# Splitting the expert weights earlier and later in a cross-attention and mixture-of-experts kernel

## The reference

```python
x = x + xattn(layernorm(x), ctx, ctx, mask, Wq, Wk, Wv, Wo)   # 16 heads of 8, softmax over 64 keys
flat = layernorm(x).reshape(2048, 128)
top_scores, top_idx = top_k(flat @ router_w.T + router_bias, 2)
combine[n, top_idx] = softmax(top_scores)
up, gate = einsum('nd,kde->nke', flat, up_proj), einsum('nd,kde->nke', flat, gate_proj)
down = einsum('nke,ked->nkd', silu(gate) * up, down_proj)
x = x + einsum('nk,nkd->nd', combine, down) + (silu(flat @ sh_gate.T) * (flat @ sh_up.T)) @ sh_down.T
```

## Time and profile before

| | us |
|---|---|
| median of 3 runs | 188.59 (188.44 to 189.77) |
| the profiled execution, its own time | 188.98 |
| its span, first to last instruction | 187.2 |
| PE busy | 168.3 (90%) |
| DVE busy | 162.1 (87%) |
| ACT busy | 123.4 (66%) |
| POOL busy | 81.0 (43%) |

### The profile page before, as it was taken

The page is one execution under the profiler, slowest core; times in us unless marked ns, Lnnn a source line. Parts: engine busy times, 40 slices in busy tenths (PEclk is TensorE's granted clock), DMA queues, the critical chain, the costliest instruction groups (busy, mean ns, idle before and its releaser), DMA issues.

```text
span 187.2 us, 4388 instructions
## 1 busy us (share of the span) xinstructions
PE 168.3 (90%) x1512; PEld 131.6 (70%) x1512; DVE 162.1 (87%) x436; ACT 123.4 (66%) x282; POOL 81.0 (43%) x145
## 2 busy tenths in 40 slices
PE   7586798998989899889999989999999999999962
PEld 7554556665767677666777668888888878888841
DVE  6899999698989999988992998998998899889961
ACT  2293567686888888888889566475566555665531
POOL 5765993558688888797663523030000000000000
PEclk9999999999999999999999999999999999999995
DMA  5997700000000000001400222422554254614401
GB/s 135 315 242 187 298 12 4 2 4 2 4 0 4 0 5 0 4 0 59 158 23 0 60 105 73 121 102 87 138 173 124 71 139 127 157 72 142 81 0 56
DMA packets 13060, 15.37 MB, mean 82 GB/s; under 512 B 1520, under 2 KB 8048, under 8 KB 12912
## 3 DMA queue, kind: packets, MB, share of 16 engines
q1 hardware_dynamic: 12608, 14.57, 26.6%
q10 hardware_dynamic: 432, 0.55, 1.2%
HBM read 13.93 MB, written 1.18 MB: 81 GB/s over the span
## 4 chain that ended last, share of the span: by engine, by line
PE 39%; DVE 32%; ACT 10%; POOL 10%; issue 6%; DMA 2%; DVEq 0%; ACTq 0%
PE bank L1105 31%; DVE prob L804 5%; DVE smax L802 5%; PE bank L1058 4%; ACT prob L564 3%; POOL k_blk L435 3%; DVE v_all L842 3%; DVE xn L704 3%; POOL w_lo L462 2%; DVE xn L700 2%; DVE hid L880 2%; POOL rstd L469 2%; DVE stats L690 2%; DMA x_sb<-x 2%; ACT hid_hi L634 2%
## 5 line engine op out<-in xcount | busy, mean ns | idle before, releaser
L625 ACT ACTIVATE sig<-bank 128x512 f32<-128x512 f32 x36 | 21.6, 600 | 21.8 <-PE bank L1105 21.4
L1105 PE MATMUL bank<-xt_hi,w_hi 128*128 128x512 f32 (+1 forms) x72 | 29.2, 406 | 0.0
L1105 PE MATMUL bank<-xt_lo,w_hi 128*128 128x512 f32 (+1 forms) x72 | 28.4, 394 | 0.0
L1105 PE MATMUL bank<-xt_hi,w_lo 128*128 128x512 f32 (+1 forms) x72 | 28.2, 391 | 0.0
L863 DVE TENSOR_TENSOR hid_u<-sig,bank 128x512 f32<-128x512 f32 x32 | 21.9, 685 | 4.3 <-PE bank L1105 3.1
L804 DVE TENSOR_TENSOR prob<-bank,smax 128x512 f32<-128x512 f32 x32 | 22.1, 692 | 1.1
L1058 PE MATMUL bank<-k_blk,q_blk 64*128 64x256 f32 x128 | 18.1, 402 | 5.3 <-POOL k_blk L435 4.7
L559 ACT COPY prob_t<-bank 128x512 f32<-128x512 f32 x32 | 17.3, 589 | 8.3 <-PE bank L1034 8.3
L802 DVE TENSOR_REDUCE smax<-bank 128x8 f32<-128x512 f32 x32 | 21.8, 681 | 0.8 <-PE bank L1058 0.8
L564 ACT ACTIVATE prob<-prob 128x512 f32<-128x512 f32 x32 | 20.1, 628 | 1.1 <-DVE prob L804 0.7
L872 DVE TENSOR_TENSOR hid_lo<-hid,hid_hi 128x512 fp32r<-128x512 f32 x24 | 16.6, 690 | 1.3 <-ACT hid_hi L634 0.5
(11 more groups left out here) (113 smaller groups left out, 383.4 us busy)
## 6 DMA issues: line engine op xcount, KB each, us to landing
mix_all<-w_rows SPq DMA_DIRECT2D x64, 128.0 KB, 3.0
w_moe_sb<-w_moe SPq DMA_DIRECT2D x1, 1728.0 KB, 10.3
x_sb<-x SPq DMA_DIRECT2D x4, 256.0 KB, 7.1
ctxt_sb<-ctx_t SPq DMA_DIRECT2D x4, 256.0 KB, 6.0
ctx_sb<-ctx_nat SPq DMA_DIRECT2D x4, 256.0 KB, 5.1
out<-x_sb SPq DMA_DIRECT2D x3, 256.0 KB, 2.3
w_att_sb<-w_att ACTq DMA_DIRECT2D x1, 272.0 KB, 6.4
mrow<-mask_row ACTq DMA_DIRECT2D x1, 256.0 KB, 5.2
```

The source lines that it names most:

```text
L625: nc.scalar.activation(sig[r][:, :], gate_ps[r][:, :], ACT.Silu).then_inc(s_sig, 1)
L1105: last = nc.tensor.matmul(out, w, moving, start=start and k == 0, stop=stop and k == 2)
```

## The change

The 16 pairs of a high and a low slice stay what they are, and each has one ACT and one POOL instruction as before; they stand elsewhere in the lists. ACT rounds slices 0 to 5 behind the key copy of group 2 in the projection (and waits there until the weights have landed), slices 6 and 7 behind the key copy of group 3, and slices 8 to 15 at the end of steps 0 to 7. POOL forms the low slices 0 to 5 behind the blocks of tile 1, 6 and 7 in step 0, 8 to 10 in step 14, 11 to 13 in step 15, and 14 and 15 behind the last but one `norm2`. The waits for the last queries and keys move behind the first six low slices. PE's, DVE's and SP's lists stay as they are.

```diff
--- before.py
+++ after.py
@@ -264,6 +264,7 @@
 
 
         LEAD = -1
+        FIRST_LOW = 6
         STEPS = 4
 
         def peel(step, t):
@@ -452,8 +453,6 @@
                     rstd1_of(g + 1)
             q_block(1, 1, first=True)
             k_blocks(1, 1)
-            pool.wait_ge(s_q_sb, GROUPS)
-            pool.wait_ge(s_k_sb, GROUPS)
 
             def low_weights(t):
 
@@ -485,22 +484,34 @@
             def step(t, p, on):
                 if on(-2):
                     q_block(t + 2, p, first=False)
-                if on(1):
-                    low_weights(t - 1)
                 if on(2):
                     norm2(t - 2, p)
                 if on(-2):
                     k_blocks(t + 2, p)
+                if t == 0:
+                    for u in range(FIRST_LOW, TILES // 2):
+                        low_weights(u)
+                elif t == TILES - 2:
+                    for u in range(TILES // 2, TILES // 2 + 3):
+                        low_weights(u)
+                elif t == TILES - 1:
+                    for u in range(TILES // 2 + 3, TILES // 2 + 6):
+                        low_weights(u)
                 if on(4):
                     low_tokens(t - 4, p)
                 if t in (2 * GT + 2, 3 * GT + 2):
                     weigh_part(t // GT - 2)
 
             pool.wait_ge(s_wmoe, 16)
+            for u in range(FIRST_LOW):
+                low_weights(u)
+            pool.wait_ge(s_q_sb, GROUPS)
+            pool.wait_ge(s_k_sb, GROUPS)
             pipeline(pool, step)
             norm2(TILES - 2, 0)
+            low_weights(TILES - 2)
+            low_weights(TILES - 1)
             low_tokens(TILES - 4, 0)
-            low_weights(TILES - 1)
             low_tokens(TILES - 3, 1)
             low_tokens(TILES - 2, 0)
             norm2(TILES - 1, 1)
@@ -548,6 +559,13 @@
                 act.wait_ge(s_k, g + 1)
                 nc.scalar.copy(k_all[:, g * GT:(g + 1) * GT, :, :].rearrange("p t g s -> p g t s"),
                                k_ps[:, :].rearrange("p (g t s) -> p g t s", g=2, t=GT)).then_inc(s_k_sb, 1)
+                if g == GROUPS - 2:
+                    act.wait_ge(s_wmoe, 16)
+                    for t in range(FIRST_LOW):
+                        high_weights(t)
+                if g == GROUPS - 1:
+                    for t in range(FIRST_LOW, TILES // 2):
+                        high_weights(t)
             mask_ctx(0)
 
             def high_weights(t):
@@ -606,8 +624,8 @@
                     weights_to_sbuf(0)
                 if on(-1):
                     exponentials(t + 1, q, 1)
-                if t >= 0:
-                    high_weights(t)
+                if 0 <= t < TILES // 2:
+                    high_weights(t + TILES // 2)
 
             def tanh_of(part):
 
@@ -650,7 +668,6 @@
                 if isinstance(g, int) and (g, m) == (1, 2):
                     weights_to_sbuf(2)
 
-            act.wait_ge(s_wmoe, 16)
             for t in range(LEAD + 1, TILES - 1):
                 peel(step, t)
             t, p = TILES - 1, (TILES - 1) % 2
```

## The result

| | before | changed |
|---|---|---|
| median, us | 188.51 (188.44 to 189.77, 4 runs) | 184.11 (184.03 to 184.27, 4 runs) |
| profiled execution, us | 188.98 | 184.03 |
| its span, us | 187.2 | 182.2 |

The ratio of the runs is 0.976, with a 95% interval of 0.9736 to 0.9784: 4.4 us faster. The lines of the code moved: L1058 of before is L1074 now, L990 is L1006, L791 is L807, L769 is L785.

The account below looks back on a forecast made before the run. It took the low slice and its wait ahead of PE's keys to bound the steps, DVE the bound between its waits. 2.7 + 0.15 - 0.25 = 2.6 us off the profiled 188.98; median forecast 186.0, range 185.0 to 187.5.

Parts of the forecast that it names:

- No low slice and no wait in steps 1 to 13: Attention steps: keys no longer wait behind the low slice, DVE's six waits go, 2.7 us off the path.
- the keys keep 0.4 us of slack: Later attention steps: keys come 3.6 us after PE's scores, PE needs 4.01 for its step, so 0.4 us is spare.
- Six roundings behind group 2: Projection on ACT: 1.6 us of roundings fit the 2.25 us idle before group 3's transposes arrive, costing nothing.
- Six low slices, with 0.4 us to spare: POOL behind tile 1's blocks: 0.8 us late, covered by the rest of step 0 on PE with 0.4 to spare.
- Low slices of steps 14 and 15 and behind: POOL at the end: step 14's masks ready at 98.2, PE transposes at 99.08; later slices wanted later; cost nothing.
- Fewer roundings on ACT: End of the steps, where PE waits 0.24 us for the last exponential: 0.15 us won, between 0 and 0.24.
- A shared price: Second of the last two low slices beside DVE's subtractions and products: 0.25 us lost, at worst 0.6.
- Rival B: Last stretch: DVE stands still for a whole low slice in two meetings, 1.3 us back, 187.0 us; 10%.
- Rival A: Steps: near-equal DVE, PE and chain lose 0.1 us at new ties in 11 steps, giving 187.2 us; 20%.
- Rival C: POOL's six low slices at 30 us each lose 0.45 us, tile 2's keys 2.3 us late, 188.3 us; 5%.
- Rival D: ACT ahead of group 3 waits for weights landing late; beyond 27.2 us delays projection one for one; slower, 3%.
- Rival E: DVE's waits hid further ties: gain up to 3.6 us, time 185.0 us; 7%.

Follow-up runs that it names:

- masks_beside_keys: The changed kernel with DVE's second expert mask of steps 8 and 12 moved one half step earlier, beside POOL's keys: 185.56 us.
- slices_back: The changed kernel with POOL's low slices back ahead of norm2 in steps 1 to 15, ACT's roundings left early: 185.57 us, ratio 0.9862.
- masks_apart: The kernel before with DVE's expert masks moved from the end of steps 8 and 12 into steps 9 and 13, where POOL idles: 187.97 us.
- wait_back: The changed kernel with POOL again waiting ahead of norm2 for ACT's end-of-step signal, a one-column copy, and no slice: 185.09 us, ratio 0.9831.
- twelve_roundings: The changed kernel with 12 roundings on ACT behind the keys of group 2 in place of 6, none behind the last keys: 184.49 us.
- eight_slices_first: The changed kernel with all eight early low slices on POOL ahead of the queries of tile 2: 184.74 us, ratio 0.9797.

## Why the prediction was wrong in size

The direction and the series of wait, slice, `norm2` and keys were right; the term that failed is **"No low slice and no wait in steps 1 to 13"**. It was sized at 2.7 us and measured 4.2. Three things were left out of it:

- *A shown wait is not all that a wait costs.* The six steps with waits were sized by the 2.7 us that the earlier trace rows shows and gave 3.17. The prediction took a step of DVE as 4.32 less 0.29, so 4.03 us; it is 3.94. An `inv_den` that need not wait starts 0.08 us inside the `mv` ahead of it, and one that waits does not. Six times 0.08 is 0.48, against 0.43 measured.
- *The masks.* Steps 8 and 12 gave 0.75 and stood in no term; the prediction says of them only that they have more DVE work. In before, one mask in each stood still beside POOL's `q_blk`; `masks_beside_keys` and `slices_back` bring it back, in both steps. `masks_apart` takes 0.52 from these two steps, though a kernel with late keys can't keep all of it.
- *Waits below what the list shows.* Steps 3, 7, 9, 13 and 14 gave 0.28 in all, without a wait of DVE in the list of before. Half of it is step 7: its `inv_den` begins at 67.10, 0.05 after the end of `mv` and 0.03 after the end of PE's L990 (67.07), as behind a wait that is shown. The same distance behind L990 stands in 3 and 13 (0.06 and 0.02 us). The 0.02 of step 9 are the length of L751, and the 0.04 of step 14 have no cause that is shown.

One more step of it was wrong, and it was luck that it cost nothing: **"the keys keep 0.4 us of slack"**. They keep none. The prediction took the end of `mv` as 1.29 us after the scores from a step whose scores were 0.28 late themselves. Without that lateness it is 1.63 (55.01 to 56.64). With 0.08 until `norm2`, 2.18 from there to the end of the keys, and 0.05 to the scores, the loop takes 3.94 us, just as long as DVE's own step. In `wait_back` 0.27 us more in this loop made step 2 longer by 0.28.

Point by point:

- *PE's 4.7 us are not the gain; DVE's waits are.* Right in kind: PE's wait fell by 4.2 us and DVE's by 2.7, all that it had. That the gain came out near PE's number is chance, by the three parts above.
- *Wait, slice, `norm2` and keys one behind the other.* Right: neither half alone costs more than 1.5 of the 4.4 us, and one reordered line removes about half.
- *Six roundings behind group 2: nothing.* Right. "Without that cover all 1.6 us would be on the path" was wrong: `twelve_roundings` went 0.86 beyond it and paid 0.3 to 0.4.
- *Six low slices, with 0.4 us to spare.* Right, 0.65 to spare (slices of 0.61 in a row, not 0.64). Two more ahead of the queries cost 0.6, so the split in six and two matters.
- *Low slices of steps 14 and 15 and behind: nothing.* Right. The masks of step 14 are weighed at 93.92, and PE transposes them at 94.65; no wait of PE names a low slice.
- *Fewer roundings on ACT, 0.15.* It is there, 0.17, for the reason that the prediction gave second: ACT came late behind POOL's `bias`. The roundings have no part in it, since `masks_apart` keeps them and wins 0.16 at the same place. The wait that PE shows is no measure of it: 0.24 in the earlier trace rows, and 0.22 now:

```profile
...
93.35 0.66 PE L1050 MATMUL bank<-consts_sb,prob 128*128 128x128 f32 x4 [0.22 <-ACT prob L582]
...
```

- *A shared price, 0.25 lost.* There too, 0.20, but in another instruction: `gap` beside the first of the last two slices. The products of L896 lose nothing new. Three of them take 0.95 or 0.96 us, as three did before; the earlier trace rows gives the longest and not how many there were, and "once" was read into it. Rival B wanted two meetings of 0.64 each; there is one of 0.20.
- *Rival A, new ties among three equal engines:* the tie is there, between DVE and the loop through POOL and PE, but no sum of small waits came of it; DVE has none from 38 to 95 us. *Rival C, slow slices at 30 us:* 0.61 each. *Rival D, late weights:* landed 1.6 us early; what a late landing would do was not tried. *Rival E, more than this:* this came true in kind, by waits that the list did not show, and its bound of 3.6 was too low, since it left out the masks.
- *What the profile after would show:* the steps take 3.9 to 4.3 us in place of 4.0 to 4.1, and the last scores begin 4.35 us earlier (87.77 for 92.12), not 2.5 to 2.9; POOL's wait for `w_hi` is gone as forecast, and PE's for the keys is at its bound of 0.5.

The meetings that the rows above show end the same way: a DVE mask with two inputs in SBUF (0.21 us alone) ends 0.07 to 0.09 after POOL's instruction beside it, whether that is 0.45, 0.6 or 1.04 us long. The Trainium skill (SBUF — State Buffer, "SBUF: two separate sides") says that the two engines exclude one another there for a whole instruction, and the traces agree. The same section counts DVE instructions in a two-port mode among those that lock. The one-input scalings of L751 and the conversion of L786 behave so; that they run in such a mode is not shown. The prediction took the rule as a warning against the change; its larger effect was in the change's favour: steps 8 and 12 are 0.75 us shorter with the masks' meetings nearly gone, against 0.20 lost in `gap`.

## What to carry to other kernels

When an engine both waits for a signal and does its own work ahead of something that another engine needs, look at when the signal comes against the next input of that list: two waits that end together plus the work between them are paid in series, and moving the work behind the urgent instruction gave about half of the gain here, for one line. When the waits are gone, look at the distances that stay: an input that always arrives just before its use has no slack, though no wait is shown. Size a bound engine's step from a stretch of it without any wait, not from a step less its shown waits. In such a step, look at which SBUF-only instructions of DVE meet POOL's, before the change and where it will put them.

## What was not expected of the hardware

DVE's scalings of L751, which read a single tile of 128 x 4 and write it to SBUF, are held up by POOL like the masks (0.85 us for 0.31), and so is the conversion of L786 (0.66 for 0.17). A wait that the profile shows as 0.26 us costs 0.33 (step 5), because an unhindered `inv_den` starts 0.08 us before `mv` ends. In the profiled executions of before and of `masks_beside_keys`, PE's granted clock fell to 0.50 in the last 6 us of the span (last digits 5, and 8 and 5, of the row of the clock). In those of `slices_back` and `eight_slices_first` only the last digit is lower (8 and 7), and in the other five it is 9. A 256-column product took 0.42 in place of 0.28 us in before, 0.74 us of span in all, with the same work ahead of it as in the changed kernel. What makes the clock fall in one execution and not in the other is open.
